# An opening with transposes between the products and row sums, and products of ones with the identity in TensorE's queue

## The chip, the cores and the metric

One core of a Trainium2 chip runs the whole kernel. The metric is the device time of one execution in microseconds (us); of several executions the median is taken. The core's engines are TensorE (PE in the profile, PEld for its weight loads), VectorE (DVE), ScalarE (ACT), GpSimd (POOL) and SyncE (SP), which here only issues transfers.

## The reference

x has 16 batches of 1024 nodes with 128 features, adj is a 1024 x 1024 matrix. There are two layers:

```
h = relu(layernorm(x));  x = x + adj @ (h @ w0) + b0                 # layer 0
h = relu(layernorm(x));  x = x + gated(h)                             # layer 1
gated: five times, with m = adj @ h:
   av = [m, m];  u = h @ u3.T + u3_b
   z = sigmoid(av @ w3.T + w3_b + u);  r = sigmoid(av @ w4.T + w4_b + u)
   hv = tanh(av @ w5.T + w5_b + (r*h) @ u5.T + u5_b)
   h = (1 - z)*h + z*hv
```

## The kernel before

Every f32 operand of a large product is held as two f16 numbers, a rounded one (hi) and the remainder (lo). A product is then three f16 matmuls: hi with hi, lo with hi, hi with lo. The rounding is ScalarE's work, the remainder VectorE's. Before rounding, adj is scaled by a power of two that is found from its largest element, and w0 from its own.

The 16 batches are treated in four groups of 4, each group in two slots of 2 batches. For layer 1 the product with adj is done with seven half-size products instead of eight (blocks K_A0, K_S1, K_S2, K_A1, K_S3, K_B1, K_S4, made of quarters of adj and of sums of quarters). In layer 0 of the first group (p = 0) the plain product is used, one for each batch and half of the nodes: direct_product(g, q), g the slot, q = 0 to 3 (batch q // 2, rows of nodes q % 2). It needs the quarters K_A0 and K_A1 of adj (upper rows) for even q, K_Y12 and K_S4 (lower rows) for odd q.

The opening goes like this. SP issues the load of x for slot 0 (1 MB, both batches), eight loads of adj, 512 KB each, then x for slot 1. ScalarE's queue issues w0; once the fourth adj block has landed also five weight matrices, five bias vectors and b0 (L934 to L940). VectorE takes the statistics of 16 blocks of x (statistics0, L1345), then the largest element of each adj block (block_top, L1253), then top_factors (L1260 to L1283): the maxima of adj and w0 over all partitions. For that it writes both maxima as diagonals (top_diag), TensorE multiplies ones with them (L805), VectorE reduces the result and works out the scales. POOL works out mean and reciprocal deviation from the statistics (moments, L359 to L386). ScalarE normalises (L979) and rounds the normalised x (round_n, L999), VectorE makes its remainder (rest_n, L1381).

Adj must be transposed. TensorE turns it in units of four 128 x 128 blocks (L659); unit n goes into bank n % 5 of ps_adj. ScalarE rounds the unit out of the bank with the scale (round_rows, L946) and VectorE writes the remainder (rest_rows, L1307); only then is the bank free. A unit here is one block row j of adj, and its result lies in a strip of 128 columns across all four blocks of t_hi and t_lo, so a direct product, which uses t_hi and t_lo by block, waits for all four units of a quarter. The eight quarters are turned in the order T_ORDER: K_A0, K_A1, K_Y12, K_S4, K_S1, K_S2, K_S3, K_B1. The last four are row sums that VectorE makes first (sum_rows, L1290 to L1300, 2048 elements each).

Each engine works through its own queue in the order in which layer(0, 0) lists the calls, and waits at semaphores. For TensorE that is: all units of a quarter, then a direct product (24 matmuls), in the order q = 0, 2, 3, 1, until transpose_weights (L668). layer(0, 1) follows with direct_product(1, 0) and then layer_out (L795 to L797), the product with w0, which needs the remainders of the turned weights (L1336, L1338).

Of the kernel before, what the change touches and what calls it, by code (L numbers as in the profile page):

```python
# [5 lines left out]
def gnn_kernel(nc, x, adj, w0, b0, w3, b3, u3, c3, w4, b4, w5, b5, u5, c5, out):  # L6
# [7 lines left out]
    P = 128  # L14
# [24 lines left out]
    DIRECT = ((0, K_A0, K_A1), (2, K_A0, K_A1), (3, K_Y12, K_S4), (1, K_Y12, K_S4))  # L39
    DIRECT_RANK = {0: 0, 2: 1, 3: 2, 1: 3}  # L40
# [17 lines left out]
    NEWTON_STEPS = 3  # L58
    MOMENT_OPS = 6 + 4 * NEWTON_STEPS
# [8 lines left out]
    with ctx:  # L68
# [104 lines left out]

        def direct_bank(g, q):
            return (ps_a, ps_b, ps_c)[(DIRECT_RANK[q] + g) % 3]

# [9 lines left out]
        top_ready = sem("top_ready")  # L186
        w_op = sem("w_op")
# [140 lines left out]
        def made_direct(g, q):  # L328
            return KS * (g + 1) if DIRECT_RANK[q] == 3 else KS * g + DIRECT_RANK[q] + 1

# [15 lines left out]
        def moments(e, p, layer, slot):  # L346

            n, op = n_layer(p, slot), moment_op[layer]
            c = MOMENT_OPS * n
            st, v, t, r, g = stats[slot], var_eps[slot], newton[slot], rstd[slot], gap[slot]  # L350
# [5 lines left out]
            e.wait_ge(stats_done[layer], n + 1)  # L356


            e.tensor_tensor(mean[slot][:, :], st[:, :, 1], st[:, :, 4], op=ALU.add)  # L359
# [4 lines left out]
            e.tensor_scalar(mean[slot][:, :], mean[slot][:, :], -0.5, None, ALU.mult)  # L364
# [21 lines left out]
            e.tensor_tensor(shift[slot][:, :], mean[slot][:, :], r[:, :], op=ALU.mult).then_inc(op, 1)  # L386
# [55 lines left out]
        def _(sp):  # L442
# [127 lines left out]
        def _(pool):  # L570
# [56 lines left out]
            moments(pool, 0, 0, 0)  # L627
            bias_x(0, 0)
            moments(pool, 0, 0, 1)
# [15 lines left out]
        def _(pe):  # L645
            pe.wait_ge(ident_done, 2)

            def transpose_rows(k, js=range(HB)):
                for j in js:
                    unit = HB * T_RANK[k] + j  # L650
                    if k in T_SUMMED:
                        pe.wait_ge(t_sum_done, T_SUMMED[k])
                    else:
                        pe.wait_ge(adj_in_done[j + (HB if k in (K_Y12, K_S4) else 0)], 16)
                    if unit >= len(ps_adj):
                        pe.wait_ge(t_hi_done, unit - len(ps_adj) + 1)
                        pe.wait_ge(t_lo_done, unit - len(ps_adj) + 1)
# [1122 lines left out]
```

## Time and profile before

| | us |
|---|---|
| median of 3 runs | 1473.76 |
| lowest, highest | 1472.54, 1473.83 |
| profiled execution, own time | 1472.45 |
| its span | 1470.7 |
| TensorE busy | 1442.9 |
| VectorE busy | 1232.7 |
| ScalarE busy | 936.1 |
| POOL busy | 205.8 |

The span runs from the first to the last instruction; the profiled execution's own time has a little around it. All durations and dates used below are from this one execution. Dates are counted from the span's start. A TensorE instruction's duration reaches beyond the start of the next, as matmuls are pipelined; the distance from start to start is what one costs.

### The profile page before, as it was taken

What the parts mean: (1) busy time and instruction counts of PE and PEld (TensorE: products, weight loads), DVE (VectorE), ACT (ScalarE), POOL (GpSimd) and SP (SyncE); (2) the same over time, 40 slices, a digit from 0 to 9 for tenths busy, and PEclk for the clock granted to TensorE, in tenths of its full rate; (3) what the DMA queues carried; (4) which work ended last, traced back from release to release, by engine and by line L of the source; (5) the groups of instructions that cost most, each with busy time, mean ns of one, the idle gap of its engine ahead of it and who ended that gap; (6) DMA issues with size and microseconds to landing.
All of it is one profiled execution on the core that took longest, in us unless ns stands there. A gap on an engine that the chain in (4) does not pass through costs nothing.

```text
span 1470.7 us, 20051 instructions
## 1 busy us (share of the span) xinstructions
PE 1442.9 (98%) x7015; PEld 673.0 (46%) x7015; DVE 1232.7 (84%) x1717; ACT 936.1 (64%) x1448; POOL 205.8 (14%) x369
## 2 busy tenths in 40 slices
PE   5999999999999999999999999999999999999999
PEld 3653444444444444444444444444444444444444
DVE  7989788888789888898778988889778888887778
ACT  4656666667568566776567666676665865556654
POOL 2440012400230004040203000422021100000000
PEclk9999999999999999999999999999999999999999
DMA  7213423371633333463522343346263232333323
GB/s 218 30 33 64 91 51 87 60 95 31 79 76 58 82 58 64 123 76 65 62 59 57 61 94 68 81 85 86 40 79 87 45 64 51 57 88 65 65 58 86
DMA packets 333155, 105.83 MB, mean 72 GB/s; under 512 B 310400, under 2 KB 327680, under 8 KB 333056
## 3 DMA queue, kind: packets, MB, share of 16 engines
q1 hardware_dynamic: 314816, 95.49, 32.0%
q0 software_dynamic: 16512, 8.39, 5.5%
q8 instruction: 58, 0.95, 0.3%
q10 hardware_dynamic: 1728, 0.66, 0.2%
q14 instruction: 41, 0.34, 0.1%
HBM read 13.24 MB, written 8.39 MB: 15 GB/s over the span
## 4 chain that ended last, share of the span: by engine, by line
PE 90%; DVE 6%; ACT 2%; issue 1%; DMA 1%; ACTq 0%; SPq 0%; DVEq 0%
PE ps_a L676 30%; PE ps_c L676 15%; PE ps_b L676 7%; PE ps_u L760 7%; PE ps_u L764 7%; PE ps_u L762 7%; PE ps_v L760 4%; PE ps_v L762 4%; PE ps_v L764 4%; PE ps_a L714 1%; PE ps_b L714 1%; PE ps_c L714 1%; DVE rh L1429 1%; DVE rh L1425 1%; DVE h_lo L1436 1%
## 5 line engine op out<-in xcount | busy, mean ns | idle before, releaser
L676 PE MATMUL ps_a<-t_hi,nx_hi 128*128 128x512 f16 x576 | 218.3, 379 | 1.3 <-ACT rh L1026 1.3
L676 PE MATMUL ps_a<-t_lo,nx_hi 128*128 128x512 f16 x576 | 218.3, 379 | 0.0
L676 PE MATMUL ps_a<-t_hi,nx_lo 128*128 128x512 f16 x576 | 218.3, 379 | 0.0
L1044 ACT ACTIVATE rh<-ps_v,bias,w_inv 128x512 f32<-128x512 f32 x160 | 123.9, 778 | 84.4 <-PE ps_v L764 84.4
L1040 ACT ACTIVATE m_hi<-rh 128x512 f16<-128x512 f32 x138 | 86.4, 628 | 112.0 <-DVE rh L1412 111.6
L1464 DVE TENSOR_TENSOR rh<-rh,area 128x512 f32<-128x512 f32 x160 | 109.7, 696 | 54.3 <-ACT rh L1049 50.7
L1026 ACT ACTIVATE rh<-ps_a 128x512 f32<-128x512 f32 x138 | 81.4, 590 | 109.0 <-PE ps_a L676 100.8
L1049 ACT ACTIVATE rh<-ps_u,bias,w_inv 128x512 f32<-128x512 f32 x160 | 120.1, 773 | 20.7 <-PE ps_u L764 19.0
L1057 ACT ACTIVATE area<-ps_u,bias,w_inv 128x512 f32<-128x512 f32 x160 | 122.0, 771 | 16.9 <-PE ps_u L764 16.9
L1425 DVE SCALAR_TENSOR_TENSOR rh<-rh,area 128x1024 f32<-128x1024 f32 x78 | 95.4, 1223 | 43.9 <-ACT rh L1044 43.5
L1468 DVE TENSOR_TENSOR rh_lo<-rh,rh_hi 128x512 f16<-128x512 f32 x160 | 109.9, 688 | 20.1 <-ACT rh_hi L1062 17.8
L1004 ACT ACTIVATE h_hi<-area 128x1024 f16<-128x1024 f32 x78 | 82.3, 1055 | 68.8 <-DVE area L1431 68.8
L760 PE MATMUL ps_u<-m_hi,w_hi 128*128 128x512 f16 x320 | 121.3, 379 | 2.5 <-DVE m_lo L1419 2.5
L1419 DVE SCALAR_TENSOR_TENSOR m_lo<-rh,m_hi 128x512 f16<-128x512 f32 x138 | 95.0, 692 | 33.2 <-ACT m_hi L1040 28.0
L764 PE MATMUL ps_u<-m_hi,w_lo 128*128 128x512 f16 x320 | 121.3, 379 | 0.0
L762 PE MATMUL ps_u<-m_lo,w_hi 128*128 128x512 f16 x320 | 121.3, 379 | 0.0
L676 PE MATMUL ps_c<-t_lo,nx_hi 128*128 128x512 f16 x288 | 109.2, 379 | 0.0
L676 PE MATMUL ps_c<-t_hi,nx_lo 128*128 128x512 f16 x288 | 109.2, 379 | 0.0
L676 PE MATMUL ps_c<-t_hi,nx_hi 128*128 128x512 f16 x288 | 109.1, 379 | 0.0
L1062 ACT ACTIVATE rh_hi<-rh 128x512 f16<-128x512 f32 x160 | 99.6, 625 | 10.7 <-DVE rh L1464 7.4
L359 POOL TENSOR_TENSOR mean<-stats 128x16 f32<-128x16 f32 x14 | 13.2, 943 | 662.1 <-DVE stats L1345 517.0
L1429 DVE TENSOR_TENSOR rh<-rh,area 128x1024 f32<-128x1024 f32 x78 | 95.8, 1228 | 8.5 <-DVE rh L1425 0.5
(245 smaller groups left out, 3147.0 us busy)
## 6 DMA issues: line engine op xcount, KB each, us to landing
xr<-in_x_dram SPq DMA_DIRECT2D x6, 1024.0 KB, 5.1
xr<-b_rows POOLq DMA_DIRECT2D x6, 1024.0 KB, 14.4
out_dram<-xr SPq DMA_DIRECT2D x5, 1024.0 KB, 4.2
area<-in_adj_dram SPq DMA_DIRECT2D x8, 512.0 KB, 8.4
nx_hi<-s SPq DMA_TRANSPOSE x128, 2.4
nx_lo<-s SPq DMA_TRANSPOSE x128, 2.5
area<-in_x_dram SPq DMA_DIRECT2D x2, 1024.0 KB, 5.4
area<-b_rows POOLq DMA_DIRECT2D x2, 1024.0 KB, 13.9
```

The source lines that it names most:

```text
L676: last = nc.tensor.matmul(o[:, :], a[:, PLACE[k], j, :], b[:, k, j, :], start=(opens and j == 0 and n == 0), stop=(j == HB - 1 and n == 2) ...
L760: nc.tensor.matmul(bank_out[:, :], w_hi[:, w, :], a_hi[:, q, :], start=start, stop=False, skip_group_check=reopen)
L762: nc.tensor.matmul(bank_out[:, :], w_hi[:, w, :], a_lo[:, q, :], start=False, stop=False, skip_group_check=reopen)
L764: return nc.tensor.matmul(bank_out[:, :], w_lo[:, w, :], a_hi[:, q, :], start=False, stop=stop, skip_group_check=reopen)
L1044: nc.scalar.activation(cand[:, q, :], V_BANK[q][:, :], ACT.Tanh, bias=bias[:, BV:BV + 1], scale=w_inv[:, CAND:CAND + 1]).then_inc(cand_rea ...
L1049: nc.scalar.activation(rh[:, q, :], U_BANK[q][:, :], ACT.Sigmoid, bias=bias[:, BR:BR + 1], scale=w_inv[:, GATES:GATES + 1]).then_inc(r_rea ...
L1057: nc.scalar.activation(z[:, q, :], U_BANK[q][:, :], ACT.Sigmoid, bias=bias[:, BZ:BZ + 1], scale=w_inv[:, GATES:GATES + 1]).then_inc(z_read ...
L1062: nc.scalar.activation(rh_hi[:, q, :], rh[:, q, :], ACT.Copy).then_inc(rh_hi_done, 1)
L1425: nc.vector.scalar_tensor_tensor(out=cand[part], in0=cand[part], scalar=SCALE16, in1=h[slot][part], op0=ALU.mult, op1=ALU.subtract).then_i ...
L1429: nc.vector.tensor_mul(cand[part], cand[part], z[part]).then_inc(zdiff_done, 1)
L1464: nc.vector.tensor_mul(rh[:, q, :], rh[:, q, :], h[slot][:, q, :]).then_inc(rh_done, 1)
L1468: nc.vector.tensor_sub(rh_lo[:, q, :], rh[:, q, :], rh_hi[:, q, :]).then_inc(rh_lo_done, 1)
```

## The change

It touches the opening (p = 0) alone.

- Loads: x for slot 0 comes as two loads, its first batch before adj, its second behind adj. The bias vectors and b0 are issued by SP, once the last adj block has landed.
- Statistics and moments are taken for each batch by itself. The first batch's come first; the second batch's statistics stand behind the remainder of unit 1.
- The maximum of w0 is worked out by itself, before those of adj. Of adj's, only a diagonal of 128 columns is spread. ScalarE waits for the new semaphore top_scaled, which comes as soon as the scale is written.
- A unit is now one result block i: it is read from all four adj blocks of a quarter, and written as one block of t_hi and t_lo. A direct product waits for one unit at a time.
- direct_product takes a list of units, and behind the three matmuls of each block TensorE turns one unit. Only five units are turned before the first product.
- The order of the direct products of slot 0 is q = 0, 1, 2, 3.
- stay_awake: TensorE multiplies ones with the identity, 10 times before the spread of adj's maximum and 28 times behind it, into a part of ps_b that nobody reads.

```diff
+    DIRECT_ROWS = ((K_A0, K_A1), (K_Y12, K_S4))
+    DIRECT_ORDER = ((0, 1, 2, 3), (0, 2, 3, 1))
+    AWAKE = (10, 28)
...
-            load_x(0, 0)
+            load_first_batch(0, x_first)
             for b in range(BLOCKS):
                 sp.dma_start(adj_in[:, b, :], adj_dram[b, :, :]).then_inc(adj_in_done[b], 16)
+            load_first_batch(1, x_loaded[0])
             load_x(0, 1)
+            sp.wait_ge(adj_in_done[BLOCKS - 1], 16)
+            for n, v in enumerate((b3, c3, b4, b5, c5)):
+                sp.dma_start(bias_in[:, n:n + 1], v.rearrange("(d a) -> d a", a=1)).then_inc(biases_in, 16)
+            sp.dma_start(b0_rows[:, :], b0.partition_broadcast(P)).then_inc(b0_in, 16)
...
-            moments(pool, 0, 0, 0)
+            moments(pool, 0, 0, 0, slice(0, 1), first_moment_op, stats_first)
+            moments(pool, 0, 0, 0, slice(1, 2))
+            moments(pool, 0, 0, 1)
             bias_x(0, 0)
-            moments(pool, 0, 0, 1)
             scale_weights()
...
+            def transpose_unit(unit):
+                k, i = T_ORDER[unit // HB], unit % HB
+                if k in T_SUMMED:
+                    pe.wait_ge(t_sum_done, T_SUMMED[k])
+                elif i == 0:
+                    for j in range(HB):
+                        pe.wait_ge(adj_in_done[j + (HB if k in (K_Y12, K_S4) else 0)], 16)
+                if unit >= len(ps_adj):
+                    pe.wait_ge(t_hi_done, unit - len(ps_adj) + 1)
+                    pe.wait_ge(t_lo_done, unit - len(ps_adj) + 1)
+                for j in range(HB):
+                    last = nc.tensor.transpose(ps_adj[unit % len(ps_adj)][:, j * P:(j + 1) * P],
+                                               T_ROWS[k][:, j, :, i], ident[:, :])
+                last.then_inc(adjT_done, 1)
...
+            def direct_product(g, q, turned=()):
...
+                for half, k in enumerate(DIRECT_ROWS[q % 2]):
                     for j in range(HB):
+                        pe.wait_ge(t_hi_done, HB * T_RANK[k] + j + 1)
+                        pe.wait_ge(t_lo_done, HB * T_RANK[k] + j + 1)
...
+                        if HB * half + j < len(turned):
+                            transpose_unit(turned[HB * half + j])
...
+            def stay_awake(count):
+                for _ in range(count):
+                    nc.tensor.matmul(ps_b[:, 0:P], ones[:, :], ident[:, :], start=True, stop=True)
...
+                    pe.wait_ge(w0_top_op, 2)
+                    nc.tensor.matmul(ps_c[:, P:2 * P], ones[:, :], top_diag[:, 1, :], start=True, stop=True
+                                     ).then_inc(w0_top_spread, 1)
+                    for unit in range(len(ps_adj)):
+                        transpose_unit(unit)
+                    stay_awake(AWAKE[0])
+                    pe.wait_ge(top_op, 3)
+                    pe.wait_ge(w0_top_op, 3)
+                    nc.tensor.matmul(ps_c[:, 0:P], ones[:, :], top_diag[:, 0, :], start=True, stop=True
+                                     ).then_inc(top_spread, 1)
+                    stay_awake(AWAKE[1])
+                    direct_product(0, 0, range(len(ps_adj), len(ps_adj) + 2 * HB))
+                    direct_product(0, 1, range(len(ps_adj) + 2 * HB, 4 * HB))
                     pe.wait_ge(top_op, 4)
                     direct_product(0, 2)
+                    direct_product(0, 3, range(4 * HB, 6 * HB))
                     transpose_weights()
```

ScalarE's order of calls:

```diff
-                    normalise(0, 0, 0)
-                    act.wait_ge(top_ready, 1)
-                    round_rows(K_A0)
+                    normalise(0, 0, 0, range(2))
                     round_n(0, 0, 0, 0)
-                    round_rows(K_A1)
+                    act.wait_ge(top_scaled, 1)
+                    for unit in range(3 * HB):
+                        round_unit(unit)
+                    normalise(0, 0, 0, range(2, 3))
+                    round_rows(K_S4)
+                    normalise(0, 0, 0, range(3, 4))
                     round_n(0, 0, 0, 1)
```

VectorE's order of calls:

```diff
+                    first_statistics()
+                    w0_top()
+                    for b in range(BLOCKS - 1):
                         block_top(b)
+                    w0_top_spread_max()
+                    block_top(BLOCKS - 1)
+                    adj_top()
                     top_factors()
-                    rest_rows(K_A0)
                     rest_n(0, 0, 0, 0)
+                    rest_unit(0)
+                    rest_unit(1)
+                    statistics0(0, 0, range(BLOCKS, 2 * BLOCKS))
+                    for unit in range(2, 10):
+                        rest_unit(unit)
+                    statistics0(0, 1, range(BLOCKS))
+                    statistics0(0, 1, range(BLOCKS, 2 * BLOCKS))
+                    rest_unit(10)
+                    rest_unit(11)
+                    rest_rows(K_S4)
                     rest_n(0, 0, 0, 1)
+                    sum_rows(K_S1)
+                    rest_m(g, 0)
                     sum_weights()
                     sum_biases()
+                    rest_m(g, 1)
                     rest_weights()
                     sum_rows(K_S2)
+                    rest_n(0, 0, 1, 0)
                     rest_m(g, 2)
+                    rest_rows(K_S1)
+                    rest_rows(K_S2)
                     sum_rows(K_S3)
+                    rest_n(0, 0, 1, 1)
                     rest_m(g, 3)
                     rest_turned_weights()
                     sum_rows(K_B1)
```

## Rows read from the trace of the kernel before

**Rows 1.** The page: busy times of the engines, and the chain by engine.

```profile
PE 1442.9 (98%) x7015; PEld 673.0 (46%) x7015; DVE 1232.7 (84%) x1717; ACT 936.1 (64%) x1448; POOL 205.8 (14%) x369
...
PE 90%; DVE 6%; ACT 2%; issue 1%; DMA 1%; ACTq 0%; SPq 0%; DVEq 0%
```

**Rows 2.** Busy times by stretch: bounds, length, busy time and count of each engine.

```profile
0.00:27.30 27.30, 9.31 (x34) 6.67 (x35) 18.10 (x40) 12.25 (x25) 8.07 (x31) 1.00 0.73 260
27.30:60.98 33.68, 33.68 (x189) 19.77 (x190) 32.51 (x56) 22.23 (x44) 17.63 (x37) 1.00 0.40 45
...
98.50:140.00 41.50, 37.58 (x171) 15.99 (x169) 38.96 (x47) 28.50 (x45) 9.99 (x10) 1.00 0.20 41
```

**Rows 3.** The chain in order of time, opening: start us, us, what.

```profile
15.68 0.53 ACTq L940
...
39.57 0.44 PE ps_u L659 x4
...
48.32 5.18 PE ps_a L714 x24
```

**Rows 4.** Timeline of the weight loads: start us, us, instruction, idle before.

```profile
9.70 0.72 PEld L659 LDWEIGHTS ps_u<-ident,area 128*128 128x128 f32 x4 [0.56 <-DMA area<-in_adj_dram]
10.98 1.57 PEld L659 LDWEIGHTS ps_v<-ident,area 128*128 128x128 f32 x8 [0.56 <-DMA area<-in_adj_dram]
```

**Rows 5.** Timeline of TensorE.

```profile
18.86 1.22 PE L805 MATMUL ps_c<-top_diag,ones 128*128 128x256 f32 x2 [5.91 <-DVE top_diag L1268]
24.09 2.80 PE L659 MATMUL ps_u<-ident,area 128*128 128x128 f32 x12 [4.01 <-DVE t_lo L1307]
27.30 0.38 PE L714 MATMUL ps_a<-t_hi,ny_hi 128*128 128x512 f16 x1 [0.41 <-DVE ny_lo L1381]
27.52 0.38 PE L714 MATMUL ps_a<-t_lo,ny_hi 128*128 128x512 f16 x1
```

**Rows 6.** Timeline of VectorE.

```profile
5.84 3.19 DVE L1345 BATCH_NORM_STATS2 stats<-xr 128x6 f32<-128x128 f32 x16 [5.84 <-DMA xr<-in_x_dram]
8.95 9.08 DVE L1253 TENSOR_REDUCE block_max<-area 128x1 f32<-128x1024 f32 x8
...
18.33 0.48 DVE L1268 TENSOR_SCALAR top_diag<-ident,tops 128x128 f32<-128x128 f32 x2
20.12 0.42 DVE L1271 TENSOR_REDUCE top<-ps_c 128x2 f32<-128x256 f32 x1 [1.31 <-PE ps_c L805]
...
20.86 0.16 DVE L1279 TENSOR_SCALAR top_scale<-top_exp 128x2 int32<-128x2 int32 x1
...
23.20 2.07 DVE L1307 SCALAR_TENSOR_TENSOR t_lo<-ps_u,top_scale,t_hi 128x512 f16<-128x512 f32 x3 [1.94 <-ACT t_hi L946]
...
25.93 1.23 DVE L1381 TENSOR_TENSOR ny_lo<-ysc,ny_hi 128x1024 f16<-128x1024 f32 x1
...
38.46 2.28 DVE L1290 TENSOR_TENSOR area<-area 128x2048 f32<-128x2048 f32 x1
...
62.53 0.69 DVE L1419 SCALAR_TENSOR_TENSOR m_lo<-ps_b,m_hi 128x512 f16<-128x512 f32 x1
...
83.60 0.69 DVE L1419 SCALAR_TENSOR_TENSOR m_lo<-ps_b,m_hi 128x512 f16<-128x512 f32 x1 [1.22 <-ACT m_hi L1040]
```

**Rows 7.** Timeline of POOL, the first and the last operation of moments(0, 0).

```profile
9.12 0.23 POOL L359 TENSOR_TENSOR mean<-stats 128x16 f32<-128x16 f32 x1 [7.50 <-DVE stats L1345]
...
15.95 0.22 POOL L386 TENSOR_TENSOR shift<-mean,rstd 128x16 f32<-128x16 f32 x1
```

**Rows 8.** Timeline of ScalarE.

```profile
16.33 6.26 ACT L979 ACTIVATE ysc<-xr,shift,rstd 128x128 f32<-128x128 f32 x16 [13.86 <-POOL shift L386]
22.50 1.81 ACT L946 ACTIVATE t_hi<-ps_u,top_scale 128x512 f16<-128x512 f32 x3
...
24.78 1.05 ACT L999 ACTIVATE ny_hi<-ysc 128x1024 f16<-128x1024 f32 x1
```

**Rows 9.** The chain in order of time, the kernel's end.

```profile
1463.41 0.89 PE ps_u L903 x8
```

More of the change, by code:

```diff
@@ L344, in steps_ahead, with moments @@
             return t == dt and slot == to_slot and not final(p)
[L346 to L350, printed above, removed]
+        def moments(e, p, layer, slot, batches=slice(0, 2), op=None, ready=None):
+            n = n_layer(p, slot)
+            c = 0 if op else MOMENT_OPS * n
+            blocks = slice(BLOCKS * batches.start, BLOCKS * batches.stop)
+            st, v, t, r, g, mu, sh = (a[:, blocks] for a in (stats[slot], var_eps[slot], newton[slot], rstd[slot],
+                                                             gap[slot], mean[slot], shift[slot]))
+            op = op or moment_op[layer]
             def wait_apart(done):
@@ L354, in wait_apart @@
                 e.sem_inc(moment_asked, 1)
-            e.wait_ge(stats_done[layer], n + 1)
-            e.tensor_tensor(mean[slot][:, :], st[:, :, 1], st[:, :, 4], op=ALU.add)
+            if ready:
+                e.wait_ge(ready, 1)
+            else:
+                e.wait_ge(stats_done[layer], n + 1)
+            e.tensor_tensor(mu[:, :], st[:, :, 1], st[:, :, 4], op=ALU.add)
             e.tensor_tensor(g[:, :], st[:, :, 1], st[:, :, 4], op=ALU.subtract)
@@ L716, in direct_product @@
                                                     stop=(half == 1 and j == HB - 1 and n == 2))
-                last.then_inc(prod_done, KS - 3 if DIRECT_RANK[q] == 3 else 1)
+                        if half == 1 and j == HB - 1:
+                            last.then_inc(prod_done, KS - 3 if rank == 3 else 1)
+                        if HB * half + j < len(turned):
+                            transpose_unit(turned[HB * half + j])
             def split_count(n, k):
@@ L937, in _, with round_unit, round_rows @@
                 act.dma_start(w_raw[:, k, :], w).then_inc(weights_in, 16)
[L938 to L948 removed]
+            def round_unit(unit):
+                act.wait_ge(adjT_done, unit + 1)
+                nc.scalar.activation(t_block(0, T_ORDER[unit // HB])[:, unit % HB, :], ps_adj[unit % len(ps_adj)][:, :],
+                                     ACT.Identity, scale=top_scale[:, 0:1]).then_inc(t_hi_done, 1)
+            def round_rows(k):
+                for i in range(HB):
+                    round_unit(HB * T_RANK[k] + i)
             def round_weights():
@@ L972, in normalise @@
                 n = n_layer(p, slot)
-                act.wait_ge(moment_op[layer], MOMENT_OPS * (n + 1))
+                if p == 0 and layer == 0 and slot == 0 and quarters[0] == 0:
+                    act.wait_ge(first_moment_op, MOMENT_OPS)
+                else:
+                    act.wait_ge(moment_op[layer], MOMENT_OPS * (n + 1))
                 if quarters[0] == 0:
@@ L1338, in rest_turned_weights, with statistics0 @@
                 nc.vector.tensor_sub(w_lo[:, 5, :], ps_c[:, 0:D], w_hi[:, 5, :]).then_inc(w_lo_done, 1)
-            def statistics0(p, slot):
+            def statistics0(p, slot, blocks=range(2 * BLOCKS)):
                 n = n_layer(p, slot)
@@ L1343, in statistics0, with first_statistics @@
                 dve.wait_ge(x_loaded[n % 4], 16 * (n // 4 + 1))
-                for b in range(2 * BLOCKS):
+                for b in blocks:
                     last = nc.vector.bn_stats(stats[slot][:, b, :], source[:, b, :])
-                last.then_inc(stats_done[0], 1)
+                if blocks[-1] == 2 * BLOCKS - 1:
+                    last.then_inc(stats_done[0], 1)
+            def first_statistics():
+                dve.wait_ge(x_first, 16)
+                for b in range(BLOCKS):
+                    last = nc.vector.bn_stats(stats[0][:, b, :], xr[0][:, b, :])
+                last.then_inc(stats_first, 1)
             def layer_sum(p, slot):
```

158 lines of the change are left out of this document (62 added, 96 removed).

## The prediction

> **What bounds the kernel now.** Start with the page. TensorE is busy for 98% of the span and 90% of the chain that ended last is TensorE's [rows 1]. Such a kernel gets shorter only where TensorE stands still, so the next view is the table of stretches. Up to 27.30 us TensorE works for 9.31 us; from 27.30 to 60.98 it works for all of 33.68 us; from 98.50 to 140.00 it misses 3.9 us [rows 2]. The change edits only the first two of these, so the ceiling of the gain is what can be had before 27.30.
>
> The third view is the chain, for what sets 27.30. ScalarE's queue issues transfers up to 16.21, normalises 16 blocks one after another, rounds, VectorE makes four remainders and ny_lo, and the first product starts at 27.30 [rows 3]. VectorE runs beside it without a gap from 8.95 to 18.8 (block maxima, then the diagonals), so the scale would come only some 1.3 us earlier than ScalarE is ready for it (about 21.0 against 22.5) even with ScalarE free [rows 6, 8]. Both lines have to shorten, and the change shortens both. From 27.30 on nobody makes TensorE wait, until the first weight products (layer_out) at 60.98. I therefore carry two dates forward: when the first direct product starts, S, and when layer_out starts. The gain is 60.98 minus the new date of the latter.
>
> **Part by part: up to the scale.** Adjacency blocks land every 1.28 us: TensorE gets the third at 9.70 and the fourth at 10.98 [rows 4]. A half load of x has as many bytes as one block, so with half of x ahead of them all blocks land 1.28 us earlier: the fourth at 9.70, the eighth at about 14.9 (10.98 + 4 x 1.28 - 1.28 = 14.8, and a tenth or three for the weights that share the engines). The first half of x lands at 5.84 - 1.28 = 4.56.
> VectorE: 8 statistics at half of 3.19 us to 6.2; the two operations on w0, 0.5, to 6.7; maxima at 1.13 each, soon waiting for each block. The eighth can start at about 15.15 (the seventh lands at 13.55, takes 1.13, the reduction of w0's spread takes 0.3) and ends at 16.35; the two short operations behind it bring the diagonal at 16.9, against 18.81 before [rows 6]. ScalarE: the six small transfers leave its queue (5 x 0.48 + 0.53 = 2.9 us), the five weight transfers end at 12.1. POOL's moments take 7.05 us from the statistics (9.12 to 16.17 before [rows 7]) and so end at 13.3; eight normalisations, half of 6.26, end at 16.45 and rounding (1.05) at 17.6 [rows 8]. That is before the scale, so ScalarE no longer sets the start. TensorE's spread of the diagonal took 1.22 us for 256 columns [rows 5]; half the columns at the higher clock take 0.4. With VectorE's three short operations (0.8 us, 20.12 to 20.9 before) the scale is there at 18.1. VectorE: ny_lo to 19.6, two remainders at 0.67 to 20.4 and 21.0. The data of the first product are thus there at 20.4, 6.9 us earlier than before.
>
> **Part by part: ones times the identity.** The 28 products stand in TensorE's queue between the spread and the first product, and it can't skip them. Their price is the choice on which the forecast rests. The trace has the same form at the end, f32, 128 columns, not a transpose: L903 is 4 products and shows 8 instructions in 0.89 us, so one is two passes and costs 0.22 us [rows 9]. 28 of them are 6.2 us. The lower bound is one pass each, 0.11, as for a transpose (4 in 0.44 [rows 3]): 3.1 us. The upper bound is the low clock: 12 transposes took 2.80 us at 24.09 [rows 5], (2.80 - 0.42) / 11 = 0.22 a pass, so 0.44 each, 12.3 us. I take 0.22, the row of the same form. The clock should be high by then: TensorE turns 20 times from 9.70 and goes straight into ten such products, over 5 us of work, where before 2.8 us of transposes from 24.09 were followed by products that came at 0.216 us per 512 columns, the 2.4 GHz level, from their first one at 27.30 [rows 5]. The ten end by 16.0 to 16.5, under the wait for the diagonal, and cost nothing; if the clock rose only behind them they would end at 18.5 (20 transposes of 0.22 and ten products of 0.44 from 9.70) and delay all by 1.5.
> So S = 16.95 + 0.25 + 6.2 = 23.4: 3.9 us earlier than 27.30, but 3.0 us later than its data.
>
> Here the Trainium skill speaks against the transposes: "TensorE: Matmul & The Clock Gate", Part 4, says that transposes do not count as work for the clock gate. By that rule the ten products would run at the low clock, the spread would go at about 18.5 and S would be 24.9. The trace speaks the other way: nothing but transposes ran between 24.09 and 27.30, after 4.0 us of idling, and the product behind them was at full rate from the start.
>
> **From S to layer_out.** The two first products are 48 matmuls, each group of 24 in 5.18 us, with 11 transposed units of 0.44 between them [rows 3]: 23.4 + 10.4 + 4.8 = 38.6. ScalarE (0.57 a unit) and VectorE (0.67) keep up with 1.09 us a unit; the 8 and 16 statistics on VectorE (1.6 and 3.2 us [rows 6]) fit in front of TensorE because it comes late. The third product needs the second batch: ScalarE has the last unit at 35.5, is free at 36.2, normalises the last four blocks (1.6), rounds (1.05) and VectorE subtracts (1.2): 40.0. TensorE stands for 1.4 us. This wait is new. Behind it: product (0,2) 5.2, product (0,3) with 8 units 8.7, the weights 0.55, product (1,0) 5.2: 59.6.
> VectorE has from 40.0 to the end of the turned weights' remainder: three row sums (2.28 each [rows 6]) 6.8, four remainders of m 2.6, eight units 5.3, two of ny_lo 2.3, weights and biases 2.3, the turned weights 0.85: 20.2 with the gaps, so 60.2. layer_out starts at 60.2, not at 60.98: a gain of 0.8 us. The same from the other side: before, 8 of the 24 units were turned ahead of 27.30, now only 5 are, so the busy stretch grows from 33.68 to 34.8, by 1.1. Of the 3.9 us of S, 1.1 go there, 1.4 into the new wait, 0.6 into the wait of layer_out; 0.8 are left.
> VectorE then has its last row sum, to 62.4; it had 62.53 before, and 1.22 us of waiting at 83.60 for the last of the products [rows 6]. TensorE's 0.8 us survive this. The weights' scaling on POOL ends at about 51.5, needed at 54. The transfers moved to SP start when the last block has landed, about 15, with nothing behind them on SP until the first turn of layer 1; the biases are first needed at 44.
> Behind 83.6 the orders are unchanged and everything shifts alike; I add nothing for it.
>
> **The sum.** The profiled execution was 1472.45 us (span 1470.7): 1471.65. It lies 1.3 below the median 1473.76, which is what is compared: 1473.0.
>
> **Rivals.** (a) The dummy products are no wall: one pass each, or otherwise over by 20.4. Then S is 20.4, but the 8 statistics stand before the third remainder and TensorE waits for it at 23.3; the twelfth unit comes at 29.9, not 32.2. Gain 0.8 + 2.3 = 3.1: 1470.7. For it: the data are there by my own sum. Against: L903's double count [rows 9].
> (b) The clock is at its lower level during the 28 (it falls in the wait for the diagonal, or had not risen). S = 16.95 + 0.45 + 12.3 = 29.7, a loss of 6.3 - 0.8 = 5.5: 1479.3. It decides from S above 24.2. For it: at 18.86, after 5.9 us of idling, a spread ran at the low rate [rows 5]. Against: the idling is now about 1 us.
> (c) VectorE becomes the bound: behind the third product ScalarE's 8 normalisations (3.2) stand before the eight units, and VectorE takes them at TensorE's 1.09 instead of 0.67 (3.4); its margin is 1.3. 5.3 - 0.8 = 4.5 late: 1478.3. Against: my sum has the units turned 3 us before VectorE comes to them.
> (d) The transposes do not lift the clock, the ten products run at 0.44 each to 18.5, and only the 28 are quick: S = 24.9, a loss of 0.7, 1474.5, counted as no change. Against: the first product at 27.30 was quick behind transposes alone [rows 5]. This is what the rule of the Trainium skill named above would do here.
>
> **How the numbers follow.** The forecast has 0.5, (a) 0.27, (b) 0.07, (c) 0.08, (d) 0.08. About 0.2% (2.9 us) can be told from no change. (a) is just beyond it, the forecast and (d) are inside: faster 0.27, same 0.58, slower 0.15. The range takes in (a) with 1 us for an earlier last block, and half the way to (c): 1469.4 to 1475.8. The likeliest case alone has 1471.8 to 1474.6 (S by 0.6 either way, and the 1.4 us wait there or not).
>
> **What would show it.** Right: 76 instructions of the line with ones and ident, 56 of them back to back over about 6.2 us, and the first direct product the moment they end, near 23.4, while its data were ready about 3 us before; a wait of TensorE of 1 to 2 us before the third product, released by ny_lo; layer_out near 60. Wrong: the first product released by VectorE or ScalarE instead (a), the 56 over 10 us or more (b), TensorE standing at a transpose of the later units or at layer_out (c). If VectorE's diagonal isn't at 16.9 within 0.7, my dates of the transfers are off.

## The result, and the profile after

| us | before | after |
|---|---|---|
| median | 1473.06 (20 runs) | 1475.44 (20 runs) |
| lowest, highest | 1472.44, 1474.09 | 1474.85, 1476.90 |
| profiled execution, own time | 1472.45 | 1476.62 |
| its span | 1470.7 | 1474.6 |

The ratio after to before is 1.0017, with a 95% interval of 1.001 to 1.0023: slower by 2.4 us, where 0.8 us of gain was forecast. The time lies in the range given, 1469.4 to 1475.8, and outside the 1471.8 to 1474.6 of the likeliest case alone. Its direction is the wrong one, and the loss is larger than its uncertainty.

The runs of after fall in two groups: 14 at 1474.85 to 1475.70, with a recorded TensorE clock of 1.000, and 6 at 1476.62 to 1476.90, with 0.998 or 0.999, the profiled execution among them.

The page of after, its first line and the chain by engine, against [rows 1]:

```profile
PE 1451.3 (98%) x7093; PEld 684.2 (46%) x7093; DVE 1232.8 (84%) x1718; ACT 937.0 (64%) x1448; POOL 209.2 (14%) x392
...
PE 87%; DVE 6%; ACT 2%; issue 1%; DMA 0%; DVEq 0%
```

TensorE has 8.4 us more of busy time, 6.42 of them the 28 products behind the spread (TensorE's one product of ones with adj's maximum, at 17.10 below). The table of stretches against [rows 2] (bounds, length, busy time and count of PE, PEld, DVE, ACT and POOL, then the granted clock, DMA share and GB/s):

```profile
0.00:23.00 23.00, 13.69 (x94) 13.28 (x95) 17.27 (x39) 8.53 (x15) 5.63 (x32) 1.00 0.83 303
23.00:60.98 37.98, 36.06 (x209) 22.80 (x207) 31.73 (x54) 27.52 (x53) 22.90 (x60) 1.00 0.25 28
60.98:84.72 23.74, 21.91 (x146) 14.43 (x147) 21.39 (x55) 11.49 (x22) 6.79 (x10) 0.93 0.53 62
```

Before, TensorE had no idle time from 27.30 to 60.98; now 1.9 us are missing in the second stretch, 1.8 more in the third, and in the third the granted clock is 0.93. TensorE's timeline of the opening, against [rows 5] (start us, us, instruction, idle before and its releaser):

```profile
10.07 2.80 PE L686 MATMUL ps_u<-ident,area 128*128 128x128 f32 x12 [2.16 <-DMA area<-in_adj_dram]
12.66 1.91 PE L686 MATMUL ps_v<-ident,area 128*128 128x128 f32 x8
14.37 2.75 PE L836 MATMUL ps_b<-ident,ones 128*128 128x128 f32 x20
17.10 0.49 PE L848 MATMUL ps_c<-top_diag,ones 128*128 128x128 f32 x2
17.43 6.42 PE L836 MATMUL ps_b<-ident,ones 128*128 128x128 f32 x56
23.68 0.38 PE L745 MATMUL ps_a<-t_hi,ny_hi 128*128 128x512 f16 x1
...
40.87 0.38 PE L745 MATMUL ps_c<-t_hi,ny_hi 128*128 128x512 f16 x1 [1.70 <-issue]
...
62.81 0.22 PE L829 MATMUL ps_v<-w_hi,m_hi 128*128 128x128 f16 x1 [2.04 <-issue]
...
63.03 0.31 PE L829 MATMUL ps_v<-w_hi,m_hi 128*128 128x128 f16 x1
63.14 0.31 PE L830 MATMUL ps_v<-w_lo,m_hi 128*128 128x128 f16 x1
...
67.00 0.22 PE L830 MATMUL ps_u<-w_lo,m_hi 128*128 128x128 f16 x1
67.05 0.22 PE L831 MATMUL ps_u<-w_hi,m_lo 128*128 128x128 f16 x1
67.11 0.38 PE L745 MATMUL ps_c<-t_hi,ny_hi 128*128 128x512 f16 x1
```

Up to 23.68 the dates are as forecast: 56 instructions in a row, the first direct product the moment they end, no releaser beside it. Then three things to see. The wait before the third product (1.70). The wait of 2.04 us before layer_out at 62.81. And the steps behind that wait: 0.11 us from start to start at 63.03, 0.056 at 67.00. So layer_out, 48 matmuls, takes 4.30 us (62.81 to 67.11); before it took 2.68 (60.98 to 63.66).

Both waits are put down to "issue": TensorE waits for several semaphores, and the profile names none. VectorE's timeline names them by its dates:

```profile
39.44 1.23 DVE L1442 TENSOR_TENSOR ny_lo<-ysc,ny_hi 128x1024 f16<-128x1024 f32 x1 [1.61 <-ACT ny_hi L1039]
...
60.09 1.22 DVE L1442 TENSOR_TENSOR ny_lo<-ysc,ny_hi 128x1024 f16<-128x1024 f32 x1 [1.34 <-ACT ny_hi L1039]
61.23 0.68 DVE L1480 SCALAR_TENSOR_TENSOR m_lo<-ps_a,m_hi 128x512 f16<-128x512 f32 x1
61.83 0.68 DVE L1390 TENSOR_TENSOR w_lo<-ps_v,w_hi 128x512 f16<-128x512 f32 x1
62.43 0.28 DVE L1392 TENSOR_TENSOR w_lo<-ps_c,w_hi 128x128 f16<-128x128 f32 x1
```

The remainders of the turned weights (L1390, L1392) end at 62.71, and layer_out starts at 62.81. They stand behind rest_n(0, 0, 1, 1) (L1442), for which VectorE idles 1.34 us. That one waits for ScalarE, whose timeline says why it is late:

```profile
55.07 0.69 ACT L980 ACTIVATE t_hi<-ps_v,top_scale 128x512 f16<-128x512 f32 x1 [0.43 <-PE ps_v L686]
55.66 3.18 ACT L1019 ACTIVATE ysc<-xr,shift,rstd 128x128 f32<-128x128 f32 x8
58.93 1.06 ACT L1039 ACTIVATE ny_hi<-ysc 128x1024 f16<-128x1024 f32 x1
59.89 0.58 ACT L1080 ACTIVATE m_hi<-ps_a 128x512 f16<-128x512 f32 x1
60.37 0.59 ACT L994 ACTIVATE w_hi<-ps_v 128x512 f16<-128x512 f32 x1
```

The last unit is rounded at 55.07 to 55.76. Behind it the queue holds eight normalisations and their rounding, which layer_out does not need, and only then the rounding of the turned weights, which it does.

Granted clock by stretch, same columns as the stretches above:

```profile
63.00:64.00 1.00, 1.00 (x13) 1.00 (x11) 1.00 (x1) 0.00 (x0) 0.00 (x0) 0.50 1.26 136
...
66.00:67.00 1.00, 1.00 (x19) 1.00 (x17) 1.00 (x3) 0.00 (x0) 0.00 (x0) 0.85 1.29 143
```

0.50 is 1.2 GHz: after the 2.04 us of idling TensorE runs for some 3.5 us at the lower level, which costs 1.6 us in this execution.

One more wait is new, far behind. The table of TensorE's waits from 84 us on has one group that differs, here after:

```profile
PE ps_u L794 <- DVE m_lo L1480: 3.1, 6, 0.6
```

Before it is 2.5 us in 5 waits. The sixth, at 1452.77, is shown in the last section. The profiled executions then differ by 1.83 (date of layer_out), 1.62 (its rate) and 0.6 (that wait), 4.05 us; the spans differ by 3.9.

### The profile page after: what moved, and what is told of

Same layout as the page of the kernel before. It is cut to its first block, busy times and chain, and to the rows that moved or that the text cites. A ratio compares the mean times of both kernels' runs of the same rounds, so it can differ in the third digit from the quotient of the medians.

```text
span 1474.6 us, 20287 instructions
## 1 busy us (share of the span) xinstructions
PE 1451.3 (98%) x7093; PEld 684.2 (46%) x7093; DVE 1232.8 (84%) x1718; ACT 937.0 (64%) x1448; POOL 209.2 (14%) x392
## 4 chain that ended last, share of the span: by engine, by line
PE 87%; DVE 6%; ACT 2%; issue 1%; DMA 0%; DVEq 0%
PE ps_a L707 29%; PE ps_c L707 15%; PE ps_b L707 7%; PE ps_u L794 7%; PE ps_u L798 7%; PE ps_u L796 7%; PE ps_v L794 4%; PE ps_v L798 4%; PE ps_v L796 4%; DVE h_lo L1497 1%; DVE rh L1490 1%; DVE rh L1486 1%; DVE area L1465 1%; DVE nx_lo L1442 0%; DVE m_lo L1480 0%
## 5 line engine op out<-in xcount | busy, mean ns | idle before, releaser
L1097 ACT ACTIVATE area<-ps_u,bias,w_inv 128x512 f32<-128x512 f32 x160 | 121.8, 770 | 16.9 <-PE ps_u L798 16.9
L375 POOL TENSOR_TENSOR mean<-stats 128x16 f32<-128x16 f32 (+1 forms) x15 | 13.4, 893 | 664.5 <-DVE stats L1399 514.8
```

Source lines behind the costliest of these rows:

```text
L1097: nc.scalar.activation(z[:, q, :], U_BANK[q][:, :], ACT.Sigmoid, bias=bias[:, BZ:BZ + 1], scale=w_inv[:, GATES:GATES + 1]).then_inc(z_read ...
```

## The experiments

Theory A: the 28 products are a wall; each one less gives its time back. Theory C: layer_out is set by the order of ScalarE's queue, not by the amount of VectorE's work. Theory B, the rival in two of the expectations, is that VectorE's own work sets it. Each experiment's "before" is the one measured with it: 1472.81 for e1 to e4, 1473.34 for e5 to e8, 1472.95 for e9. The three groups ran on different chips, so a difference of medians across groups can be off by some 0.5 us; such differences are read beside the dates of the profiles.

**e1 and e2: fewer products behind the spread.**

```diff
-    AWAKE = (10, 28)
+    AWAKE = (10, 14)     # e1
+    AWAKE = (10, 0)      # e2
```

> The changed kernel with 14 instead of 28 products of ones with the identity behind the spread of adj's maximum. Theory A (the products are a wall in TensorE's queue at 0.11 us a pass, and everything up to layer_out hangs on the first direct product): the first product starts at 17.4 + 3.1 = 20.6 instead of 23.7, the last unit of K_S2 is turned about 2.3 us earlier than 54.4, layer_out starts near 60.4 instead of 62.8, and the time falls by 2.0 to 2.6 us, to about 1473.0. Theory B (VectorE's own work sets layer_out; TensorE's start is hidden): the first product is earlier as in A, but layer_out stays within 0.5 us of 62.8 and the time within 0.5 us of 1475.4.

> The changed kernel with none of the 28 products (the ten before the spread stay). TensorE idles from 17.4 until the first product's data are there. Theory A: the data are there at about 20.4, so the first product starts there, as with 14; if the granted clock stays at its upper level the time is that of 14 products (1473.0), and if the 3 us of idling bring it down the first products cost 0.43 us per 512 columns for some us, and 1 to 2 us are given back (1474 to 1475). Theory B: no change against 1475.4 either way.

e1: 1473.15 us median (1471.66 to 1473.49, 11 runs), ratio to before 0.9998 (0.9989 to 1.0006). It has the same two groups as after: five runs at 1471.66 to 1471.86 with clock 1.000, six at 1473.15 to 1473.49 with 0.998 or 0.999. In dates everything moved by 2.6 us, the third product from 40.87 to 38.25 and layer_out from 62.81 to 60.17, with the same wait in front of it:

```profile
60.17 0.22 PE L829 MATMUL ps_v<-w_hi,m_hi 128*128 128x128 f16 x1 [2.05 <-issue]
```

So A holds up to layer_out, and B is out: 14 products less give back 2.6 of their 3.2 us; the rest goes to a wait of 0.52 us for t_lo in the first product, behind the eight statistics. The median falls by 2.3 us, but it lies in the upper group here and in the lower one in after. Group against group it is 3.5 us (1471.76 against 1475.24): 2.6 of date, 0.6 of the late wait, which e1 does not have, and about 0.3 that is not accounted for. Theory C's wait follows unchanged, since ScalarE's queue moved with the rest.

e2: 1472.16 us (1471.72 to 1475.61, 11 runs), ratio 1.0 (0.9991 to 1.0009). The first product can't start earlier than in e1, because its data are not there (first fence: TensorE's timeline of e2; second: its stretch, columns as before):

```profile
20.46 0.38 PE L745 MATMUL ps_a<-t_hi,ny_hi 128*128 128x512 f16 x1 [3.05 <-DVE t_lo L1358]
...
21.11 0.78 PE L686 MATMUL ps_u<-ident,area 128*128 128x128 f32 x4
21.69 0.63 PE L745 MATMUL ps_a<-t_hi,ny_hi 128*128 128x512 f16 x1
```

```profile
17.40:24.00 6.60, 3.55 (x16) 2.41 (x16) 6.45 (x20) 3.69 (x6) 1.14 (x6) 0.80 0.47 133
```

The first three matmuls are quick (0.22 from start to start); from the transposes at 21.11 on TensorE steps at half that rate, the 1.2 GHz level, for some 3.5 us. This execution fell to that level once more behind its wait before layer_out, as after did, so its 65.34 in the table below holds both. Not in all runs: six lie at 1471.7 to 1472.2, the slowest five reach from 1472.65 to 1475.61.

**e3: after, with the turned weights ahead of the normalisation (Theory C).** Calls that stay are the lines without a sign.

```diff
 # ScalarE
                     round_rows(K_S2)
-                    normalise(0, 0, 1, range(2, 4))
-                    round_n(0, 0, 1, 1)
                     round_m(g, 3)
                     round_turned_weights()
+                    normalise(0, 0, 1, range(2, 4))
+                    round_n(0, 0, 1, 1)
 # VectorE
                     rest_rows(K_S2)
-                    sum_rows(K_S3)
-                    rest_n(0, 0, 1, 1)
                     rest_m(g, 3)
                     rest_turned_weights()
+                    sum_rows(K_S3)
                     sum_rows(K_B1)
+                    rest_n(0, 0, 1, 1)
```

> The changed kernel with 28 products, but ScalarE rounds m of (0,3) and the turned weights before it normalises the second half of slot 1, and VectorE makes their remainders before the row sums K_S3, K_B1 and the last ny_lo. Theory C (layer_out is late because ScalarE's 3.2 us of normalising, 1.1 of rounding and VectorE's operations in order behind them stand before the weights' remainder): the remainder is written at about 58 instead of 62.7, TensorE goes from product (1,0) into layer_out at 60.6 without a wait, no part of layer_out runs at 1.2 GHz, and the time falls by about 2 us against the changed kernel's quick runs, to 1473.2, with no runs near 1476.8 any more. Rival (POOL's scaling of the weights, or VectorE as the bound all the way to layer 1): the wait only moves to the transposes of K_S3 or to the next product, and the time stays at 1475 to 1475.5.

1473.22 us (1473.00 to 1473.45, 11 runs), ratio 1.0002 (0.9993 to 1.0011): 2.2 us better than after. VectorE's timeline and TensorE's:

```profile
56.92 0.68 DVE L1390 TENSOR_TENSOR w_lo<-ps_v,w_hi 128x512 f16<-128x512 f32 x1
57.52 0.28 DVE L1392 TENSOR_TENSOR w_lo<-ps_c,w_hi 128x128 f16<-128x128 f32 x1
```

```profile
60.46 0.22 PE L829 MATMUL ps_v<-w_hi,m_hi 128*128 128x128 f16 x1
60.52 0.22 PE L830 MATMUL ps_v<-w_lo,m_hi 128*128 128x128 f16 x1
```

The weights are there at 57.8, 2.7 us ahead of their use, the wait is gone, the steps are 0.056 us from the first matmul on, and the 11 runs lie within 0.45 us, all with a recorded clock of 1.000: the upper group of after has gone with the wait. Against the 14 quick runs of after (1475.24 at their median) the gain is 2.0 us. No work was taken away and the amount on VectorE is the same, so it is the order that set layer_out, as Theory C says. The edit moved calls on both engines, on VectorE a row sum (2.28 us) and ny_lo (1.22) too; neither half was run alone. An estimate from the rows of after: with VectorE's half alone the weights come from ScalarE at 61.1 as before, and with ScalarE's half alone their remainders still stand behind ny_lo, so neither would end the wait.

**e4: e3 with AWAKE = (10, 14).**

> Both edits together, 14 products and the weights first. If A and C are both right and independent, the gains add: 2.3 + 2.2, a time near 1470.9, 2 us below the kernel before. If either gain only fills a slack that the other leaves, the time is that of the better one alone, about 1473.

1469.98 us (1469.76 to 1470.05, 11 runs), ratio 0.9979 (0.997 to 0.9988), layer_out at 58.02 with no wait. The gains add. The time is 0.9 us below the 1470.9 expected, and 0.8 of that is the late wait, which e3 has (3.3 us in 6 waits for m_lo) and e4 has not (2.5 in 5). It beats before by 2.8 us and after by 5.5. What is left of waits: 0.53 us for t_lo at 23.27, 1.70 before the third product at 38.29, and 0.24 before the product behind layer_out at 61.10, where the ny_lo that was moved back now ends at 60.89.

**e9: e4 with AWAKE = (10, 0).** What does the cover behind the spread bring in this order?

> e4 with none of the 14 products of ones with the identity behind the spread (the ten before it stay): what does that cover bring by itself, in the order that gained most? Theory: the data of the first product are ready at the same date, near 20.4 us, so nothing starts sooner without the 14; TensorE stands for about 3 us behind the spread instead, and what is at stake is only the rate behind that wait. Where the first matmuls come 0.43 us apart for about 4 us, as in e2's profile, some 9 of them cost 0.2 us more each, of which the wait of 0.5 us for t_lo takes up a part: +1 to +1.7 us in those executions, none in the others. So 1470.0 to 1471.6 over the runs, median near 1470.8, and a wider spread than e4's 0.3 us. Rival: the products' only effect is to fill the time, the clock comes back at once: 1470.0, as e4, with a spread as small. Second rival: the remaining weight loads and reads of ones and ident disturb nothing and the 14 held back the first product: 1469.5 or less.

1470.18 us (1469.96 to 1472.36, 11 runs), ratio 0.9984 (0.9975 to 0.9993). Six runs lie within 0.2 us of e4's median, four at 1470.84 to 1471.19, one at 1472.36. In the profiled execution, one of the six, the matmuls behind the wait are quick (start to start 0.22):

```profile
20.66 0.38 PE L745 MATMUL ps_a<-t_hi,ny_hi 128*128 128x512 f16 x1 [3.05 <-DVE t_lo L1358]
20.88 0.38 PE L745 MATMUL ps_a<-t_lo,ny_hi 128*128 128x512 f16 x1
```

The theory's two kinds of execution are there; that most are of the quick kind is what the rival said. At the median the 14 products bring nothing that can be told: 0.2 us, between runs on different chips. The first product of this profile is 0.25 us later than e4's, but not for want of the 14: the ten products ahead of the spread reached the upper rate only at 15.9 and held the spread until 17.22, where e4's went at 16.87. What the 14 bring is against single executions, five of the 11, that are 0.9 to 2.4 us above e4's median.

**e7: e4 with AWAKE = (0, 0).**

> Against weights_first_awake14 (1469.98): no products of ones with the identity at all, neither the ten nor the 14. The queue does not get shorter by it, since the data of the first product are there at 20.4 either way. My theory: without them TensorE idles from about 14 to 16.9 and from 17.3 to 20.4, the granted clock is at 1.2 GHz for the first products in most runs, and those runs take 1 to 2.5 us longer, with a wide spread: median 1471 to 1472.5. Rival (the products buy nothing): 1470.0 with the narrow spread of before.

1471.72 us (1471.01 to 1472.51, 11 runs), ratio 0.9989 (0.998 to 0.9998): 1.7 us over e4 and 1.5 over e9 (1.2 us each, if every kernel is taken against the before of its own group; the dates behind layer_out differ by 2.0 and 1.7). Beside e9, the ten products ahead of the spread bring 1.2 to 1.7 us. A kernel with the 14 and without the ten was not run. TensorE's timeline:

```profile
16.98 0.80 PE L848 MATMUL ps_c<-top_diag,ones 128*128 128x128 f32 x2 [2.62 <-DVE top_diag L1318]
20.84 0.58 PE L745 MATMUL ps_a<-t_hi,ny_hi 128*128 128x512 f16 x1 [3.06 <-DVE t_lo L1358]
21.21 0.63 PE L745 MATMUL ps_a<-t_lo,ny_hi 128*128 128x512 f16 x1
...
25.05 0.60 PE L745 MATMUL ps_a<-t_hi,ny_hi 128*128 128x512 f16 x1
25.48 0.39 PE L745 MATMUL ps_a<-t_lo,ny_hi 128*128 128x512 f16 x1
```

The spread takes 0.80 us instead of 0.39 to 0.49, and the first matmuls come 0.43 us apart until 25.48.

**e6: e4 with all of x ahead of adj.**

```diff
             load_first_batch(0, x_first)
+            load_first_batch(1, x_loaded[0])
             for b in range(BLOCKS):
                 sp.dma_start(adj_in[:, b, :], adj_dram[b, :, :]).then_inc(adj_in_done[b], 16)
-            load_first_batch(1, x_loaded[0])
```

> Against weights_first_awake14 (1469.98): both halves of x are loaded ahead of adj again, as two loads. My theory: all adj blocks land 1.28 us later, the diagonal of adj's maximum is ready at about 18.1 instead of 16.8, the first product starts near 21.7, the second batch's numbers are no earlier, and the time rises by 1.0 to 1.3 us, to about 1471.2. Rival (the wait for ny_lo of the second batch before the third product absorbs it): less than 0.4 us.

1471.36 us (1471.16 to 1471.58, 11 runs), ratio 0.9988 (0.9979 to 0.9996): 1.38 us over e4. The transposes start at 11.07 instead of 9.83, the first product at 21.74 instead of 20.41. Splitting x is worth one block's transfer, as the prediction had it (1.28).

**e8: e4 with the units in blocks again**, units 5 to 7 ahead of product (0, 0), 8 to 15 ahead of (0, 1), 16 to 23 ahead of (0, 3).

```diff
-                    direct_product(0, 0, range(len(ps_adj), len(ps_adj) + 2 * HB))
+                    for unit in range(len(ps_adj), 2 * HB):
+                        transpose_unit(unit)
+                    direct_product(0, 0)
...
```

> Against weights_first_awake14 (1469.98): the units are turned in blocks ahead of each product (5 to 7 before (0,0), 8 to 15 before (0,1), 16 to 23 before (0,3)) instead of one behind each group of three matmuls; everything else as there. TensorE's work is the same. My theory: in a block of eight TensorE outruns VectorE (0.44 against 0.67 us a unit, five banks), and before (0,3) it waits for the sum rows K_S2 and for the remainder of unit 16, which stands behind ny_lo of slot 1 in VectorE's queue (about 48.7): 2 to 4 us longer, 1472 to 1474. Rival (the distribution doesn't matter, only TensorE's total): within 0.5 us of 1470.

1478.11 us (1476.68 to 1478.41, 6 runs), ratio 1.0029 (1.0018 to 1.0041): 8.1 us over e4, in the direction expected and at twice the upper end of its size. TensorE's table of waits up to 66 us (waited for; us in total, times, longest):

```profile
PE ps_u L686 <- DVE t_lo L1364: 3.1, 2, 1.6
PE ps_u L686 <- DVE rh L1364: 3.1, 1, 3.1
```

With five banks, a block of units goes at the pace of rounding and remainder, and TensorE stands. The longest wait, up to 35.90, is one for remainders that stand behind the second batch's 16 statistics in VectorE's queue (31.93 to 35.11). The expectation left out that the wait for t_lo moves the whole first product (24.06 instead of 20.41), and the clock: it was at 0.50 from 36.41 to 39.82 and from 53.48 to 56.89, behind two of the waits, and 3.4 us at half rate cost up to 1.7 each time. Of the parts of the change that were taken back singly (this one, the split load, the products of ones), turning between the products is by far the largest in this order.

**e5: before, with the bias vectors and b0 issued by SP.** The first step of the chain in [rows 3] is ScalarE's queue of transfers. Is it a cause?

```diff
 # SP, behind load_x(0, 1)
+            sp.wait_ge(adj_in_done[BLOCKS - 1], 16)
+            for n, v in enumerate((b3, c3, b4, b5, c5)):
+                sp.dma_start(bias_in[:, n:n + 1], v.rearrange("(d a) -> d a", a=1)).then_inc(biases_in, 16)
+            sp.dma_start(b0_rows[:, :], b0.partition_broadcast(P)).then_inc(b0_in, 16)
```

(and the same transfers taken out of ScalarE's queue)

> The kernel before with one part of the change: the five bias vectors and b0 are issued by SP behind the last adj block instead of by ScalarE's queue. My theory: nothing is gained, because ScalarE's queue was through at 16.21 and POOL's last operation of the moments ended at 16.17, so the normalisation starts at 16.3 as before; time within 0.3 us of the kernel before (1472.8). The rival, the view of the chain, in which ScalarE's queue is the late step: the normalisation starts up to 2.9 us earlier and the first product by up to 1.3 us (then VectorE's scale is late), a time near 1471.5.

1472.81 us (1472.28 to 1473.38, 11 runs), ratio 0.9997 (0.9988 to 1.0006): no difference clear of noise. ScalarE's timeline (us, with its queue's issues as ACTq):

```profile
12.45 0.94 ACTq L941 DMA_DIRECT2D rh_hi<-in_L_gnn_u_w_dram  x2
16.39 6.26 ACT L980 ACTIVATE ysc<-xr,shift,rstd 128x128 f32<-128x128 f32 x16 [13.93 <-POOL shift L386]
```

The queue is empty at 13.4 and the normalisations start at 16.39 as before, when POOL's moments are there. The queue ended just then, so the chain named it; it held nothing up, and the move gains nothing by itself. In the whole change it may still be needed: there the moments come at 13.2, while the six transfers would have kept the queue until about 16.2 [rows 3], an estimate that no run tests.

**The sum over all profiles.** Call the direct product that follows layer_out the product behind it. If theories A and C are the whole of it, the date at which the product behind layer_out starts should account for each span, with the waits for m_lo far behind added:

| | product behind layer_out, us | against before | waits for m_lo against before | sum | span against before |
|---|---|---|---|---|---|
| before | 63.66 | | (2.5) | | 1470.7 |
| after | 67.11 | +3.45 | +0.6 | +4.05 | +3.9 |
| e1 | 64.48 | +0.82 | 0 | +0.8 | +0.7 |
| e2 | 65.34 | +1.68 | 0 | +1.7 | +1.7 |
| e3 | 63.55 | -0.11 | +0.8 | +0.7 | +0.6 |
| e4 | 61.10 | -2.56 | 0 | -2.6 | -2.8 |
| e5 | 64.53 | +0.87 | 0 | +0.9 | +0.9 |
| e6 | 62.44 | -1.22 | 0 | -1.2 | -1.3 |
| e7 | 63.10 | -0.56 | 0 | -0.6 | -0.6 |
| e8 | 69.37 | +5.71 | 0 | +5.7 | +5.6 |
| e9 | 61.36 | -2.30 | 0 | -2.3 | -2.4 |

It does, within 0.3 us in every row. Nothing is given back or gained between the opening and the last 30 us. The row of e5 is not its edit's doing: its first product starts at 27.37, as before's, and the matmuls are slow up to about 28.95 (last section). Such a start costs 0.8 us, about half of before's own spread of 1472.44 to 1474.09; the profiled execution of before, 1472.45, is at the fast end of it.

## Why the prediction was wrong

**What bounds the kernel, and the two dates: right.** The gain or loss is the date at which layer_out is done; the table above shows it for the ten kernels that were run, after among them, but for the late wait.

**Up to the scale: right.** Forecast and measured: first half of x 4.56 and 4.81, fourth adj block 9.70 and 10.07, the diagonal 16.9 and 17.05, data of the first product 20.4 and, where no product of ones holds it back, 20.46 (e2). e6 confirms the price of the split load.

**Ones times the identity: right; the date of the clock was luck in part.** 56 instructions take 6.42 us, 0.11 a pass, two passes a product, taken from [rows 9]. S was forecast at 23.4 and measured at 23.68. Rivals (a) and (b) are out. The rate came later than forecast. In after the 20 transposes take 0.215 us each from the first to the last (10.07 to 14.37), twice what a transpose costs later between products (four in 0.44), and the ones times the identity speed up to 0.107 a pass only from about 15.0 us. The ten end at 16.95, not by 16.0 to 16.5, just ahead of the diagonal. In e1, whose queue is the same up to there, the transposes themselves speed up:

```profile
9.77 2.80 PE L686 MATMUL ps_u<-ident,area 128*128 128x128 f32 x12 [2.14 <-DMA area<-in_adj_dram]
12.36 1.16 PE L686 MATMUL ps_v<-ident,area 128*128 128x128 f32 x8
13.35 2.40 PE L836 MATMUL ps_b<-ident,ones 128*128 128x128 f32 x20
```

The eight at 12.36 take 0.99 us from start to start, in after 1.71. From 12.6 on they come 0.11 apart, after 2.8 us in which TensorE did nothing but transposes; in e4 the same happens at 13.3. So transposes can be enough, as the prediction read [rows 5]. In the other profiles with the ten products the rate rises among those, in e8 and e9 only near 15.9. The queue is the same, so it does not fix the date. By the rule of the Trainium skill, "TensorE: Matmul & The Clock Gate", Part 4, transposes do not count for the gate. The rows of e1 and e4 do not bear that out. Rival (d), in which the ten are slow to their end at 18.5, is out too. But where the rate comes late, the ten are not hidden: in e9 they hold the spread until 17.22.

**The third product: right.** A wait of 1.4 us to 40.0 was forecast, 1.7 us to 40.87 came, released as said by the second batch's ny_lo.

**The failed step** is this: "VectorE has from 40.0 to the end of the turned weights' remainder: three row sums ... 20.2 with the gaps, so 60.2." It adds up VectorE's work and takes the sum for a date. Its durations were about right: in after VectorE works for some 20 us between the third product's ny_lo and 62.71. Its gaps were not: it idles for 2.1 us. The last items stand behind rest_n(0, 0, 1, 1), which needs ScalarE's ny_hi, and ScalarE's queue has 3.18 + 1.06 us of normalising and rounding between the last unit and that. Followed through that queue with the prediction's own numbers: third product at 40.0, 5.2 and 8.7 for the next two, so the last unit is turned at 53.9 and rounded at 54.5; eight normalisations, half of the 6.26 of [rows 8], to 57.6; rounding 1.05 to 58.7; then VectorE's rest_n 1.2, m 0.65 and weights 0.85 to 61.4. That is 0.4 us later than before, a loss and no gain, and with the third product 0.9 later than forecast it is 62.3, against 62.71 measured. The prediction's sum has no term for ScalarE's eight normalisations behind the units. Rival (c) names ScalarE's eight normalisations in front of the units, the first half of slot 1; these ran at 44.38, and the units' remainders were through at 56.46. The eight at 55.66 are the ones that count. So (c)'s sign came, TensorE standing at layer_out, but not by its mechanism nor at its price (1478.3). e3 shows the step: the same work in another order, and the wait is gone.

**Left out: what a wait costs beyond its length.** The 2.04 us at 62.81 cost another 1.6 where the clock fell behind it, in 6 of 20 runs of after and 6 of 11 of e1, the two kernels with that wait and the cover behind the spread. The wait is longer than the one the prediction allowed itself there (0.6), and its place, ahead of 48 short matmuls, is the same. In e3, e4 and e6, which have the cover and not that wait, all 33 runs have clock 1.000, and the runs of each lie within 0.45 us.

**"Everything shifts alike" behind 83.6: nearly right.** It holds in all rows of the table but two, after and e3, which have a late wait of 0.6 to 0.8 us more.

So the 14 runs at full clock have spans of 1473.0 to 1473.6, some 2.4 us or more over before's 1470.7: 1.83 of date and 0.6 of the late wait. Their median, 1475.24, is 2.2 over the median of before, which lies 0.6 above before's profiled execution; what spreads before's executions enters there. Of the median's 2.4 the other 0.2 comes from the six.

That the time fell into the range at all is luck: the range reached up to 1475.8 for the sake of half of rival (c), which did not come.

## What to carry to other kernels

Work added up on one engine is no date. Before a date is taken from such a sum, follow the last item back through the queue of the engine that feeds it, and ask what stands there that the waiting engine doesn't need: here a few calls moved behind it were worth 2.2 us, and turned a loss into a gain with half of the covering products. Work that only fills a wait should end when the data come: the 14 products too many held everything back by 2.6 us. The cover behind the spread was worth nothing clear at the median, and 0.9 to 2.4 us in five executions of 11; the ten products ahead of the spread were worth 1.2 to 1.7 us.

## What the runs showed of the hardware that was not expected

The granted clock printed for a stretch does not show every slow spell. In e7 the matmuls of 512 columns come 0.43 us apart from 20.84 to 25.05, as at 1.2 GHz, and the stretch says 1.00 (columns as in the stretches above):

```profile
20.40:24.00 3.60, 3.17 (x10) 1.81 (x11) 3.60 (x12) 1.84 (x3) 0.94 (x5) 1.00 0.04 6
```

The trace of e7 has no record of the clock at all before 25.49, the date at which the steps become quick, and where there is none, 1.00 is printed. The traces of the other kernels begin their record late too (before at 27.12, after at 15.10), so for the opening the distance from start to start is the reading to go by. In e5's profile the first products behind 2.8 us of transposes came 0.43 us apart up to about 28.95 us, where those of before, behind the same transposes, were quick from 27.30 [rows 5]. So the same queue of instructions gives both; what decides between them is open.

Every profile has some 50 issues of a transposing transfer on SP, of 568, that take 1.7 to 2.6 us instead of 1.2 to 1.3. They come at uneven distances, often 23 to 30 us. This one, in after (SP's timeline, then VectorE's, then TensorE's), falls among the last transposes of the kernel, where nothing covers it:

```profile
1445.69 2.20 SPq L518 DMA_TRANSPOSE s<-h_lo  x1
1447.94 1.27 SPq L515 DMA_TRANSPOSE s<-h_hi  x1
...
1448.55 1.49 DVE L1548 SCALAR_TENSOR_TENSOR xr<-s,xr 128x512 f32<-128x512 f16 x2 [1.25 <-DMA s<-h_hi]
...
1452.77 0.38 PE L794 MATMUL ps_u<-m_hi,w_hi 128*128 128x512 f16 x1 [0.55 <-DVE m_lo L1480]
```

e3 has one at 1442.14 (2.43 us) and a wait of 0.79 us; the other profiles have none in this place and no such wait. The spans speak for a place that is tied to the kernel, as an estimate: by its date alone e3 should have 1470.6, and its 11 runs have 1471.0 to 1471.5; the 14 quick runs of after should have 1472.5 and have 1473.0 to 1473.6; e4, without the wait, should have 1468.1, and its 11 have 1467.9 to 1468.0. So it seems to come in every execution of the two kernels with 28 products, and is then a part of their price. What makes these issues long is open.
